# Windowed attention by pairs of neighbouring windows of one batch, with half the mask table and a loop of eight written-out steps

## Chip, cores and metric

One core of one Trainium2 chip runs the kernel. The metric is the device time of one execution in microseconds (us). Five engines work side by side, each through its own list of instructions: PE (TensorE: matmuls, and the weight loads shown as PEld), DVE (VectorE), ACT (ScalarE), POOL (GpSimd) and SP (SyncE, which here only issues DMAs). They order one another by semaphores.

## What is computed

The input x is (4, 32, 32, 128): four batches of 32 x 32 places with 128 channels. The first layer is a Swin block with windows of 8 x 8, shifted by 4, 16 heads of 8 channels, a rotary embedding, an additive mask per window, and a gated MLP. The second is a self-attention over all 1024 places of a batch.

```python
xw = windows(roll(layer_norm(x)))                  # 4 batches x 16 windows, 64 tokens each
q, k, v = rope(q(xw)), rope(k(xw)), v(xw)          # 16 heads of 8 channels
attn = softmax(q * scale @ k.T + attn_mask[window])   # mask depends on the window, not the batch
x = x + unroll(attn @ v @ proj_w.T + proj_b)
y = layer_norm(x)
x = x + (silu(gate(y)) * a(y)) @ fc2_w.T + fc2_b      # a, gate: halves of y @ fc1_w.T + fc1_b
f, g, h = x @ Wq + bq, x @ Wk + bk, x @ Wv + bv    # second layer, per batch, 1024 tokens
x = gamma * softmax(f @ g.T) @ h + x
```

The host rolls the image and cuts it into windows before the launch, and puts it together again after it.

## The kernel before

Two windows, 128 tokens, fill the 128 partitions; such a pair is the unit of the window attention. There are 32 pairs. Pair n holds window n // 2 of two batches (0 and 1 for an even n, 2 and 3 for an odd one). Both halves of a pair have the same window and so the same mask: `mask_f` holds the masks of all 16 windows for both directions of the scores, twice over the partitions (1,024 KB), and `mask16` is its bf16 form. A part of the mask that bf16 doesn't hold would go through two further parts of `mask16`; which of two written-out versions of PE's program runs (three parts or one) is decided by a value that PE loads at step -1, in two `pe.If` blocks. For the mask of this problem it is the second block, with one part.

**Stage 1, window attention.** Steps n = -2 to 34, one function `body(n, it, r)` for each engine (PE's has a count of mask parts besides). A step works on several pairs at once: PE projects q and k of pair n+2 (`project`, lines 748 and 750), turns q and k of pair n+1 (`turn`, line 786), writes the masks of pair n into two PSUM banks by a matmul with the identity (`masked`, line 758) and adds its scores (line 767), does masks and turned scores of pair n-1 (lines 758 and 779), multiplies pair n-3 with its values (line 843), projects v of pair n-1, and turns q of pair n once more with the row maxima in it (`t2`, line 786). DVE rotates q and k (line 941), copies the turned rows to `qk_t` (line 955), takes the row maxima (line 973), writes them as two f16 parts (lines 978 and 980) and normalises. ACT does the exponential and the f16 halves, POOL the low halves. SP sends the turned keys of the next pair to `k_t` in four DMAs, one after the other (line 717), as soon as DVE's copy is done; the scores of that pair wait for the last one (`kz_ready`).

The steps -2 to 3 are written out, the steps 4 to 27 are a hardware loop (`Fori`) of six turns of four written-out steps, and the steps 28 to 34 are written out again. In the loop an index that depends on n is a register; the mask's index is one of them, since the window is n // 2, and so is the pair that is projected. Behind the steps -1 to 3 lies the rest of the first layer norm (`ln_turn`, `ln_hi_of`, `ln_lo_of`, `ln_stats_of`, in chunks of four pairs). At the end of step -1 PE computes the bias of fc1 by 16 small matmuls (`bias`, line 444), which wait for the nine loads of REST; DVE adds to it at the start of its step 0 (line 539), and PE's step 0 begins by waiting for that.

**Loads.** SP issues three chunks of x (256 KB each), the mask table, five more chunks of x, and the nine loads of REST (line 707), of which `bv` is last.

**Stage 2, MLP.** Chunks of 512 tokens, which are four pairs. So a chunk of before has two windows of all four batches. ACT moves the result of a chunk to `x2_all` (line 578), whose layout is batch, window, token: it writes four pieces, one to each batch.

**Stage 3, second attention.** `project_fg(b, h)` (line 1356) computes the two sets of rows of half h of batch b from `x2_all`. ACT (`high_rows`, line 1641) and DVE (`rows_of`, line 1521) make them f16, and `other_half` (line 1337) sends them across the partitions: SP sends side 0 of batch 0, ACT side 1, after its `high_values`. The first scores (line 1389) wait for all four. PE's order before is fg(0,0), fg(1,0), a wait for all chunks of x2, fg(0,1), fg(1,1), then the values of batch 0 (line 1361, `project_v`).

Of the kernel before, what the change touches and what calls it, by code (L numbers as in the profile page):

```python
# [13 lines left out]
F32 = mybir.dt.float32  # L14
# [7 lines left out]
WIN, SHIFT = 8, 4  # L22
HEADS, HD = 16, 8
NWIN = (H // WIN) * (W // WIN)
WTOK = WIN * WIN
PAIRS = NWIN * B // 2
TOK = B * H * W
CHUNK = 512
CHUNKS = TOK // CHUNK
# [17 lines left out]
def at(start, size):  # L47

    return bass.ds(start, size)


def build(nc, t):
    ctx = ExitStack()
    with ctx:
# [59 lines left out]
        warm2 = sb("warm2", [128, 1])  # L114

        until_mlp = ExitStack()
        mask_f = until_mlp.enter_context(nc.sbuf_tensor("mask_f", [128, 2, NWIN, WTOK], F32))
        mask16 = until_mlp.enter_context(nc.sbuf_tensor("mask16", [128, 3, 2, NWIN, WTOK], BF16))
# [428 lines left out]
        def mlp_act(act):  # L547
# [26 lines left out]
            def body(c, u):  # L574
                if in_range(c, 2):

                    act.wait_ge(mlp_done, c - 1)
                    act.activation(x2_all[:, :, at(c * 2 - 4, 2), :],
                                   ps[:, OUT_BANK, :].rearrange("p (w b q) -> p b w q", w=2, b=B),
                                   ACT.Identity, bias=cols[:, 0:1], scale=1.0 / (WSCALE * WSCALE)).then_inc(x2_done, 1)  # L580
                if in_range(c, 1):
                    gate(c - 1, 0)
                    if isinstance(c, int) and c == 1:
                        high_of_a(2, 0)
                    gate(c - 1, 1)
# [44 lines left out]
        with ExitStack() as st:  # L630
            def tmp(name, shape, dt=F32):
                return st.enter_context(nc.sbuf_tensor(name, shape, dt))
# [9 lines left out]
            mrest = tmp("mrest", [128, 2, NWIN, WTOK])  # L642
# [17 lines left out]
            pv_ps = ps[:, PV_BANK, 0:HP * 4 * (HD + 1)].rearrange("p (h e r d) -> p h e r d", h=HP, e=2, r=2)  # L660

            FIRST, LAST = -2, PAIRS + 2
            LOOP_FROM, LOOP_TO = 4, PAIRS - 4

            LN_BANK = (PV_BANK, ST_BANK, ST_BANK + 1, PV_BANK, ST_BANK, PV_BANK, PV_BANK, PV_BANK)
            LN_BANK_FREE = (0, 0, 0, 1, 2, 4, 6, 7)
# [3 lines left out]

            def first_steps(body):
                for n in range(FIRST, 0):
                    body(n, n // 2, n % BUFS)

            def other_steps(eng, body, mlp_early):
                for n in range(0, LOOP_FROM):
                    body(n, n // 2, n % BUFS)
                with eng.Fori(LOOP_FROM // BUFS, LOOP_TO // BUFS) as it:
                    for r in range(BUFS):
                        body(it * BUFS + r, it * 2 + r // 2, r)  # L680
                for n in range(LOOP_TO, LAST + 1):
                    body(n, n // 2, n % BUFS)
                    mlp_early(LAST - n)

            def steps(eng, body, mlp_early):
# [10 lines left out]
            @block.sync  # L696
            def _(sp):
                for c in range(CHUNKS):
                    sp.dma_start(x_all[:, TPC * c:TPC * c + TPC, :],
                                 t["x"][:, TPC * c:TPC * c + TPC, :]).then_inc(x_loaded[c], 16)  # L700
                    if c == 2:

                        sp.wait_ge(qkv_loaded, 48)
                        sp.wait_ge(turn_loaded, 16)
                        sp.dma_start(mask_f[:], t["mask"]).then_inc(mask_loaded, 16)
                for dst, name in REST:
                    sp.dma_start(dst[:], t[name]).then_inc(rest_loaded, 16)
                sp.wait_ge(rows_set, 4)
                sp.wait_ge(keys_set, 1)

                def body(n, it, r):
                    if valid(n, -1):

                        sp.wait_ge(qt_ready, n + 2)
                        for j in range(4):
                            rows = slice(ROWS * j, ROWS * j + ROWS)
                            sp.dma_start(k_t[rows, (r + 1) % BUFS, j], qk_t[rows, (r + 1) % 2, 1]).then_inc(kz_ready[(r + 1) % 2], 16)

                steps(sp, body, nothing)

            @block.tensor
            def _(pe):
# [30 lines left out]
                def masked(bank, w, side, parts):  # L753

                    for part in range(parts):
                        for b in range(2):
                            mm = mask16[:, part, side, at(w, 1), :].broadcast_to([128, 8, WTOK])
                            pe.matmul(ps[:, bank + b, :].rearrange("p (h k) -> p h k", h=8), identb[:], mm,  # L758
                                      start=(part == 0), stop=False, skip_group_check=True)

                def scores(queries, keys, w, parts):

                    masked(S_BANK, w, 0, parts)
                    for c in range(4):
                        for e in range(2):
                            rows = slice(64 * e, 64 * e + 64)
                            last = pe.matmul(  # L767
                                ps[rows, S_BANK + c // 2, 256 * (c % 2):256 * (c % 2) + 256]
                                .rearrange("p (h k) -> p h k", h=4),
                                queries[:, c, rows], keys[:, :, c, rows], start=False, stop=True, skip_group_check=True)  # L770
                    return last
# [15 lines left out]
                                            ident16[:])  # L787
                    return last

                def body(n, it, r, parts):  # L790
                    u = r % 2
                    v = 1 - u

# [22 lines left out]
                    if valid(n, 0):  # L816

                        pe.wait_ge(kz_ready[u], it * 64 + 64)
                        wait(pe, mlo_done, n)
                        scores(qk_t[:, u, 0], k_t[:, r], it, parts).then_inc(s_done, 1)  # L820
                    if at_step(n, 0):
                        ln_turn(3)
                        ln_turn(4)
# [5 lines left out]
                    if valid(n, 1):  # L829

                        wait(pe, q2_ready, n)
                        wait(pe, exp_done, n - 1)
                        scores_turned(k_t[:, (r - 1) % BUFS], q_t2[:, v], it if u else it - 1, parts).then_inc(st_done, 1)
                    if at_step(n, 1):
                        ln_turn(5)
                    if valid(n, 3):
                        wait(pe, plo_done, n - 2)
                        wait(pe, norm_done, n - 3)
                        pe.wait_ge(ln_ready, CHUNKS)
                        for hp in range(HP):  # L840
                            out = pv_ps[:, hp].rearrange("p e r d -> p (e r d)")
                            for k, (p, w) in enumerate(((p_hi, v_hi), (p_hi, v_lo), (p_lo, v_hi))):
                                last = pe.matmul(out, p[:, v, 2 * hp:2 * hp + 2, :].rearrange("p h q -> p (h q)"),  # L843
                                                 w[:, v, hp].rearrange("p e r d -> p (e r d)"),
                                                 start=(k == 0 and hp == 0), stop=(k == 2), skip_group_check=True)
                        last.then_inc(pv_done, 1)
                    if valid(n, 1):
# [26 lines left out]
            def _(dve):  # L874
# [52 lines left out]

                dve.wait_ge(attn_loaded, 16 * len(ATTN))

                def body(n, it, r):  # L930
                    u = r % 2
                    v = 1 - u
                    if isinstance(n, int) and n == 0:
# [73 lines left out]
            def _(act):  # L1007
# [38 lines left out]
                ln_norm_of(2)  # L1046
                ln_hi_of(1)

                def body(n, it, r):
                    u = r % 2  # L1050
                    v = 1 - u
                    if isinstance(n, int):
# [62 lines left out]
            def _(pool):  # L1115
# [28 lines left out]

                pool.wait_ge(rows_set, 4)

                def body(n, it, r):
                    u = r % 2
                    k = (r + 2) % BUFS
                    if valid(n, -2):  # L1150
# [49 lines left out]


        until_mlp.close()
        x2_all = sb("x2_all", [128, B, NWIN, WTOK])
# [74 lines left out]
        with ExitStack() as st:  # L1278
# [31 lines left out]

            def fg_count(b, h):

                return 2 * h + b + 1 if b < 2 else 2 * b + h + 1

            def fg_bank(b, h):
                return (PV4 + 2 * b + h) if b < 2 else AUX
# [33 lines left out]
            def _(pe):  # L1350

                def tokens(b, first, count):
                    return x2_all[:, b].rearrange("p w q -> p (w q)")[:, first:first + count]
# [155 lines left out]
            def _(dve):  # L1509
# [86 lines left out]
                for h in range(2):  # L1596
                    for b in range(2):
                        rows_of(b, h)
                for h in range(2):
                    low_values(0, h)  # L1600
# [32 lines left out]
            def _(act):  # L1633
# [18 lines left out]
                for h in range(2):  # L1652
                    for b in range(2):
                        high_rows(b, h)
                high_values(0, 0)
                high_values(0, 1)
# [133 lines left out]
```

## Time and profile before

| | us |
|---|---|
| median of three runs | 422.26 |
| lowest and highest | 419.81, 424.24 |
| the profiled execution, its own time | 421.29 |
| its span from the first to the last instruction | 419.5 |
| stage 1 with its start | 0 to about 200 |
| of it the steps of the hardware loop | 50.3 to 167.6 |
| stage 2 without its overlap with stage 1 | about 200 to 288.5 |
| stage 3 | 288.5 to 419.5 |

Of the span PE is busy for 87%, DVE 73%, ACT 66% and POOL 62%. A busy share is a mean over stages with different limits; what ends a step has to be read from the step. Times below are from the start of the span.

### The profile page before, as it was taken

To read this page: it belongs to the slowest core of one execution; us is meant where nothing else is said; L and a number is where in the kernel's file an instruction comes from. 1 tells how busy PE (TensorE), PEld (TensorE's weight loads), DVE (VectorE), ACT (ScalarE), POOL (GpSimd) and SP (SyncE) were. 2 spreads that over 40 slices of the span, in tenths; PEclk is the share of its full clock that TensorE was granted. 3 is DMA by queue.
4 is the path that set the end of the run, shared out by engine and by line. 5 is a ranking of instruction groups with operands and counts; after the bars stand their busy time and mean duration, and the time that the engine had idled before them with its cause. 6 is when DMAs were issued, how large, how long until landed. Compare 5 with 4: busy or idle time off the path is not lost.

```text
span 419.5 us, 12535 instructions
## 1 busy us (share of the span) xinstructions
PE 363.6 (87%) x4732; PEld 229.6 (55%) x4732; DVE 307.5 (73%) x850; ACT 275.2 (66%) x436; POOL 259.1 (62%) x313
## 2 busy tenths in 40 slices
PE   2678799999999999978799999999269998989693
PEld 0455455666665666655355555545025766767563
DVE  8767688888888888887476666645787688784524
ACT  2758787777787778878355555455116866768581
POOL 6656476777777777886656666572006775857521
PEclk9999999999999999999899999999757999999989
DMA  6701001111000101100000000000100002010101
GB/s 199 253 22 26 18 27 27 28 28 30 26 25 25 28 26 30 29 16 3 1 2 2 0 0 0 2 0 9 45 0 15 14 19 58 3 50 2 43 11 51
DMA packets 15581, 12.53 MB, mean 30 GB/s; under 512 B 3991, under 2 KB 14136, under 8 KB 15416
## 3 DMA queue, kind: packets, MB, share of 16 engines
q1 hardware_dynamic: 14144, 11.42, 9.4%
q10 hardware_dynamic: 1400, 0.61, 0.6%
q8 instruction: 24, 0.39, 0.4%
q14 instruction: 13, 0.11, 0.1%
HBM read 4.68 MB, written 2.10 MB: 16 GB/s over the span
## 4 chain that ended last, share of the span: by engine, by line
PE 55%; DVE 20%; issue 7%; ACT 6%; POOL 4%; DMA 4%; SPq 3%; ACTq 0%; DVEq 0%; POOLq 0%
PE ps L334 8%; PE ps L1417 7%; PE ps L786 5%; PE ps L758 5%; DVE mx L1553 4%; PE ps L748 4%; PE ps L843 3%; PE ps L1361 3%; PE ps L779 3%; PE ps L767 3%; DVE ps L973 3%; POOL hl L275 2%; DVE ob L1591 2%; PE ps L750 2%; PE ps L1400 2%
## 5 line engine op out<-in xcount | busy, mean ns | idle before, releaser
L1679 POOL TENSOR_TENSOR el<-e,eh 128x1024 f16<-128x1024 f32 x28 | 59.6, 2130 | 65.2 <-ACT eh L1671 65.0
L1162 POOL TENSOR_TENSOR p_lo<-e_buf,p_hi 128x1024 f16<-128x1024 f32 x32 | 68.2, 2132 | 4.9 <-ACT p_hi L1017 3.6
L1664 ACT ACTIVATE e<-ps 128x1024 f32<-128x1024 f32 x32 | 32.7, 1023 | 39.0 <-PE ps L1406 38.7
L334 PE MATMUL ps<-y_t,fc_w 128*128 128x512 f16 x192 | 44.4, 387 | 3.7 <-POOL al L260 2.5
L1154 POOL TENSOR_TENSOR rot<-ta,tb 128x256 f32<-128x256 f32 x32 | 23.3, 728 | 38.9 <-DVE tb L941 38.7
L1553 DVE TENSOR_REDUCE mx<-ps 128x1 f32<-128x1024 f32 x32 | 39.1, 1221 | 9.9 <-PE ps L1390 9.6
L1417 PE MATMUL ps<-val,eh 128*128 128x129 f16 x512 | 37.7, 223 | 6.4 <-DVE ob L1591 5.7
L758 PE MATMUL ps<-mask,identb 128*128 (+1 forms) x128 | 39.0, 386 | 2.8 <-DMA k_t<-qk_t 2.1
L973 DVE TENSOR_REDUCE ps<-ps 128x16 f32<-128x1024 f32 x32 | 39.4, 1232 | 2.7 <-PE ps L767 1.8
L1081 ACT ACTIVATE e_buf<-ps 128x1024 f32<-128x1024 f32 x32 | 32.8, 1025 | 12.9 <-PE ps L779 12.8
L1417 PEld LDWEIGHTS ps<-val,eh 128*128 128x128 f16 x512 | 32.4, 99 | 15.0 <-issue 8.4
L456 DVE SCALAR_TENSOR_TENSOR hid<-ps,fc_bias,sg 128x512 f32<-128x512 f32 x32 | 23.9, 747 | 15.5 <-ACT sg L551 9.8
L1017 ACT ACTIVATE p_hi<-e_buf 128x1024 f16<-128x1024 f32 x32 | 33.9, 1059 | 0.8
L1671 ACT ACTIVATE eh<-e 128x1024 f16<-128x1024 f32 x32 | 33.8, 1055 | 0.7
L275 POOL TENSOR_TENSOR hl<-hid,hh 128x512 f16<-128x512 f32 x24 | 27.5, 1157 | 10.3 <-DVE yn L485 8.3
L334 PEld LDWEIGHTS ps<-y_t,fc_w 128*128 128x128 f16 x192 | 18.6, 99 | 25.2 <-POOL al L260 3.0
L748 PE MATMUL ps<-qkv_w,xn_all 128*128 128x128 f16 (+1 forms) x192 | 27.4, 252 | 4.5 <-issue 2.9
L551 ACT ACTIVATE sg<-ps,fc_bias 128x512 f32<-128x512 f32 x32 | 22.0, 689 | 13.3 <-PE ps L334 12.1
L786 PE MATMUL ps<-ident,q_rows 128*128 128x128 f16 x256 | 25.8, 224 | 4.7 <-DVE q_rows L980 3.5
L1017 ACT ACTIVATE q_t<-ps 128x512 f16<-128x512 f16 x32 | 19.1, 598 | 12.8 <-PE ps L786 12.6
L779 PEld LDWEIGHTS ps<-q_t,k_t 128*64 128x64 f16 x1024 | 18.7, 112 | 13.6 <-issue 13.6
L941 DVE TENSOR_TENSOR ta<-ps,rope 128x256 f32<-128x256 f32 x32 | 13.6, 424 | 14.3 <-PE ps L750 14.3
(158 smaller groups left out, 981.7 us busy)
## 6 DMA issues: line engine op xcount, KB each, us to landing
k_t<-qk_t SPq DMA_DIRECT2D x128, 32.0 KB, 1.8
x_all<-in_x SPq DMA_DIRECT2D x8, 256.0 KB, 5.6
out<-ob SPq DMA_DIRECT2D x8, 192.0 KB, 2.1
mask_f<-in_mask SPq DMA_DIRECT2D x1, 1024.0 KB, 4.8
yr<-xr SPq DMA_DIRECT2D x14, 64.0 KB, 2.0
fc_w<-in_fc_w SPq DMA_DIRECT2D x1, 512.0 KB, 6.8
out<-ob SPq DMA_DIRECT2D x4, 128.0 KB, 1.8
fc_w<-in_fc_w SPq DMA_DIRECT2D x1, 256.0 KB, 6.6
```

The costliest lines, as they stand in the source:

```text
L275: pool.tensor_tensor(hl[:, k, :], hid[:, k, :], hh[:, k, :], ALU.subtract).then_inc(hl_done, 1)
L334: last = pe.matmul(ps[:, bank, :], fc1_w16[:, ws, 128 * block_:128 * block_ + 128], y_t[:, v, ys, :], start=(n == 0), stop=(n == 2))
L748: pe.matmul(out, xn_all[:, at(i, 1), xs, :].rearrange("p a q -> p (a q)"), qkv_w16[:, ws, cols], start=(n == 0), stop=False, skip_group_ch ...
L758: pe.matmul(ps[:, bank + b, :].rearrange("p (h k) -> p h k", h=8), identb[:], mm, start=(part == 0), stop=False, skip_group_check=True)
L786: last = pe.transpose(out[:, c, :], rows[:, 4 * c:4 * c + 4, :].rearrange("p h r -> p (h r)"), ident16[:])
L973: dve.tensor_reduce(mx_ps, ps[:, S_BANK:S_BANK + 2, :].rearrange("p b (h k) -> p (b h) k", h=8), AX.X, ALU.max).then_inc(max_done, 1)
L1017: return act.activation(out, in_, ACT.Copy)
L1162: pool.tensor_tensor(p_lo[:, u], e_buf[:, u], p_hi[:, u], ALU.subtract).then_inc(plo_done, 1)
L1417: return pe.matmul(pv4[:, j, i, 0:DIM + 1], weights[:, T % H_BUFS, 128 * n:128 * n + 128], val[:, b % 2, part, m, 0:DIM + 1], start=first, ...
L1553: dve.tensor_reduce(mx[:, k:k + 1], two(s_bank(k)), AX.X, ALU.max, negate=True).then_inc(max4_done, 1)
L1671: act.activation(eh[:, T % H_BUFS, :], e4[:, T % E_BUFS, :], ACT.Copy).then_inc(eh_done, 1)
L1679: pool.tensor_tensor(el[:, T % H_BUFS, :], e4[:, T % E_BUFS, :], eh[:, T % H_BUFS, :], ALU.subtract).then_inc(el_done, 1)
```

## The change

A pair now holds the windows 2w and 2w+1 of one batch: pair n is batch n // 8, window pair n % 8. The mask table has eight places instead of sixteen; partitions 0 to 63 hold the mask of the even window and 64 to 127 of the odd one. Its load is 512 KB, its bf16 copy on ACT (line 1017) has 1024 elements a partition in place of 2048, and DVE's reduction over it (line 925) 512 in place of 1024.

So that the mask's index is a constant in the loop, the loop has eight written-out steps: steps -2 to 7 are written out, steps 8 to 23 are two turns of eight steps, and steps 24 to 34 are written out. This holds for all five engines, and for both versions of PE's program.

A chunk of the MLP is now 512 tokens of one batch in their order, so ACT writes one piece to `x2_all`. PE's order at the start of stage 3 becomes fg(0,0), fg(0,1), fg(1,0), the wait for all chunks, fg(1,1), and the orders of ACT, DVE and the counts follow.

```diff
-PAIRS = NWIN * B // 2
+WPAIRS = NWIN // 2
+PAIRS = WPAIRS * B
-        mask_f = until_mlp.enter_context(nc.sbuf_tensor("mask_f", [128, 2, NWIN, WTOK], F32))
+        mask_f = until_mlp.enter_context(nc.sbuf_tensor("mask_f", [128, 2, WPAIRS, WTOK], F32))
...
-                    act.activation(x2_all[:, :, at(c * 2 - 4, 2), :],
-                                   ps[:, OUT_BANK, :].rearrange("p (w b q) -> p b w q", w=2, b=B),
+                    act.activation(x2_all[:, at((c - 2) * CHUNK, CHUNK)], ps[:, OUT_BANK, :],
...
-            LOOP_FROM, LOOP_TO = 4, PAIRS - 4
+            LOOP_FROM, LOOP_TO = WPAIRS, PAIRS - WPAIRS
...
-                with eng.Fori(LOOP_FROM // BUFS, LOOP_TO // BUFS) as it:
-                    for r in range(BUFS):
-                        body(it * BUFS + r, it * 2 + r // 2, r)
+                with eng.Fori(LOOP_FROM // WPAIRS, LOOP_TO // WPAIRS) as it:
+                    for w in range(WPAIRS):
+                        body(it * WPAIRS + w, it * (WPAIRS // 2) + w // 2, w)
...
-                            mm = mask16[:, part, side, at(w, 1), :].broadcast_to([128, 8, WTOK])
+                            mm = mask16[:, part, side, w:w + 1, :].broadcast_to([128, 8, WTOK])
...
-                        scores(qk_t[:, u, 0], k_t[:, r], it, parts).then_inc(s_done, 1)
+                        scores(qk_t[:, u, 0], k_t[:, r], w, parts).then_inc(s_done, 1)
...
                 project_fg(0, 0)
+                pe.wait_ge(x1_ready, CHUNKS)
+                project_fg(0, 1)
                 pe.wait_ge(h_done, CHUNKS * HBLK)
                 project_fg(1, 0)
                 pe.wait_ge(x2_done, CHUNKS)
-                pe.wait_ge(x1_ready, CHUNKS)
-                project_fg(0, 1)
                 project_fg(1, 1)
...
-    x = x.reshape(B, nh, WIN, nw, WIN, DIM).transpose(1, 3, 0, 2, 4, 5).reshape(PAIRS, 2 * WTOK, DIM)
+    x = x.reshape(B, nh, WIN, nw, WIN, DIM).transpose(0, 1, 3, 2, 4, 5).reshape(PAIRS, 2 * WTOK, DIM)
...
-        "mask": np.concatenate([both, both], 0),
+        "mask": np.concatenate([both[:, :, 0::2], both[:, :, 1::2]], 0),
```

## Rows read from the trace of the kernel before

**Rows 1.** Windows (stretch, length, busy us of each engine, clock, DMA): the loop.
```profile
89.90:167.60 77.70, 76.39 (x1408) 48.22 (x1409) 67.36 (x176) 61.90 (x112) 58.52 (x79) 1.00 0.10 27
```

**Rows 2.** Timeline of PE (start, length): first matmuls of steps 8 to 12, 28, 29.
```profile
70.43 0.50 PE L748 MATMUL ps<-qkv_w,xn_all 128*128 128x256 f16 x3
75.27 0.50 PE L748 MATMUL ps<-qkv_w,xn_all 128*128 128x256 f16 x3
80.03 0.50 PE L748 MATMUL ps<-qkv_w,xn_all 128*128 128x256 f16 x3
84.80 0.50 PE L748 MATMUL ps<-qkv_w,xn_all 128*128 128x256 f16 x3
89.95 0.50 PE L748 MATMUL ps<-qkv_w,xn_all 128*128 128x256 f16 x3 [0.31 <-issue]
...
167.61 0.49 PE L748 MATMUL ps<-qkv_w,xn_all 128*128 128x256 f16 x3
...
172.28 0.49 PE L748 MATMUL ps<-qkv_w,xn_all 128*128 128x256 f16 x3
```

**Rows 3.** Waits in the window 70.4 to 167.6: us in total, times, longest.
```profile
PE ps L748 <- issue: 1.2, 4, 0.3
```

**Rows 4.** Timeline of PE: the mask matmuls of a loop step, then of step 29.
```profile
95.89 0.59 PE L758 MATMUL ps<-mask,identb 128*128 x2
...
173.44 0.61 PE L758 MATMUL ps<-mask,identb 128*128 128x512 bf16 x2
```

**Rows 5.** DMA queues: instruction packets of the whole span, then of 50.3 to 70.4.
```profile
q8 instruction: 24, 0.39, 0.4%
...
q8 instruction: 3, 0.05, 1.0%
```

**Rows 6.** DMA queue in 57 to 58.5, and in 63 to 65; SP's timeline; the chain.
```profile
q8 instruction: 1, 0.02, 3.9%
...
q8 instruction: 1, 0.02, 3.1%
...
57.93 1.03 SPq L717 DMA_DIRECT2D k_t<-qk_t  x1
...
63.95 2.70 DMA k_t<-qk_t
```

**Rows 7.** SP's key DMAs (line 717) in the whole span: issue time in ns, landing.
```profile
L717 SPq DMA_DIRECT2D k_t<-qk_t x128: 507/591/1633, 18.9 to 180.9; - x128
...
DMA to landing us min/median/max: 1.8/1.8/3.3
```

**Rows 8.** Waits in 50.3 to 70.4, then in 167.6 to 190.
```profile
PE ps L758 <- DMA k_t<-qk_t: 0.6, 2, 0.3
...
PE ps L758 <- DMA k_t<-qk_t: 1.0, 2, 0.5
```

**Rows 9.** The window 10 to 15; the chain from 14 to 23.2; PE's and DVE's timelines.
```profile
10.00:15.00 5.00, 3.50 (x17) 1.75 (x15) 3.37 (x7) 4.41 (x12) 3.15 (x6) 1.00 1.00 363
...
14.21 5.11 DMA bv<-in_bv
19.36 3.58 PE ps L444 x16
...
23.04 0.18 DVE fc_bias L539
...
24.62 0.80 PE L748 MATMUL ps<-qkv_w,xn_all 128*128 128x256 f16 x3 [1.69 <-issue]
...
22.54 0.38 DVE L888 BATCH_NORM_AGGREGATE mv<-stats 128x2 f32<-128x6 f32 x4
```

**Rows 10.** Waits in 18 to 25.
```profile
PE ps L444 <- DMA bv<-in_bv: 1.3, 1, 1.3
```

**Rows 11.** The chain from the end of the MLP to the first scores.
```profile
288.49 3.44 PE ps L1356 x8
...
294.32 2.26 DMA yr<-xr
```

More of the change, by code:

```diff
@@ L116, in build @@
         until_mlp = ExitStack()
-        mask_f = until_mlp.enter_context(nc.sbuf_tensor("mask_f", [128, 2, NWIN, WTOK], F32))
-        mask16 = until_mlp.enter_context(nc.sbuf_tensor("mask16", [128, 3, 2, NWIN, WTOK], BF16))
+        mask_f = until_mlp.enter_context(nc.sbuf_tensor("mask_f", [128, 2, WPAIRS, WTOK], F32))
+        mask16 = until_mlp.enter_context(nc.sbuf_tensor("mask16", [128, 3, 2, WPAIRS, WTOK], BF16))
         xn_all = until_mlp.enter_context(nc.sbuf_tensor("xn_all", [128, PAIRS, 2, 128], F16))
@@ L641, in build @@
             xn = tmp("xn", [128, 4, CHUNK])
-            mrest = tmp("mrest", [128, 2, NWIN, WTOK])
+            mrest = tmp("mrest", [128, 2, WPAIRS, WTOK])
             ta = tmp("ta", [128, 2, 2, HEADS, HD])
@@ L672, in first_steps @@
                 for n in range(FIRST, 0):
-                    body(n, n // 2, n % BUFS)
+                    body(n, n // 2, n % WPAIRS)
             def other_steps(eng, body, mlp_early):
                 for n in range(0, LOOP_FROM):
-                    body(n, n // 2, n % BUFS)
-                with eng.Fori(LOOP_FROM // BUFS, LOOP_TO // BUFS) as it:
-                    for r in range(BUFS):
-                        body(it * BUFS + r, it * 2 + r // 2, r)
+                    body(n, n // 2, n % WPAIRS)
+                with eng.Fori(LOOP_FROM // WPAIRS, LOOP_TO // WPAIRS) as it:
+                    for w in range(WPAIRS):
+                        body(it * WPAIRS + w, it * (WPAIRS // 2) + w // 2, w)
                 for n in range(LOOP_TO, LAST + 1):
-                    body(n, n // 2, n % BUFS)
+                    body(n, n // 2, n % WPAIRS)
                     mlp_early(LAST - n)
@@ L709, in _, with body @@
                 sp.wait_ge(keys_set, 1)
-                def body(n, it, r):
+                def body(n, it, w):
+                    r = w % BUFS
                     if valid(n, -1):
@@ L788, in turn, with body @@
                     return last
-                def body(n, it, r, parts):
+                def body(n, it, w, parts):
+                    r = w % BUFS
                     u = r % 2
@@ L832, in body @@
                         wait(pe, exp_done, n - 1)
-                        scores_turned(k_t[:, (r - 1) % BUFS], q_t2[:, v], it if u else it - 1, parts).then_inc(st_done, 1)
+                        scores_turned(k_t[:, (r - 1) % BUFS], q_t2[:, v], (w - 1) % WPAIRS, parts).then_inc(st_done, 1)
                     if at_step(n, 1):
@@ L841, in body @@
                             out = pv_ps[:, hp].rearrange("p e r d -> p (e r d)")
-                            for k, (p, w) in enumerate(((p_hi, v_hi), (p_hi, v_lo), (p_lo, v_hi))):
+                            for k, (p, vals) in enumerate(((p_hi, v_hi), (p_hi, v_lo), (p_lo, v_hi))):
                                 last = pe.matmul(out, p[:, v, 2 * hp:2 * hp + 2, :].rearrange("p h q -> p (h q)"),
-                                                 w[:, v, hp].rearrange("p e r d -> p (e r d)"),
+                                                 vals[:, v, hp].rearrange("p e r d -> p (e r d)"),
                                                  start=(k == 0 and hp == 0), stop=(k == 2), skip_group_check=True)
@@ L928, in _, with body @@
                 dve.wait_ge(attn_loaded, 16 * len(ATTN))
-                def body(n, it, r):
+                def body(n, it, w):
+                    r = w % BUFS
                     u = r % 2
@@ L1047, in _, with body @@
                 ln_hi_of(1)
-                def body(n, it, r):
+                def body(n, it, w):
+                    r = w % BUFS
                     u = r % 2
@@ L1145, in _, with body @@
                 pool.wait_ge(rows_set, 4)
-                def body(n, it, r):
+                def body(n, it, w):
+                    r = w % BUFS
                     u = r % 2
@@ L1202, in build @@
         until_mlp.close()
-        x2_all = sb("x2_all", [128, B, NWIN, WTOK])
+        x2_all = sb("x2_all", [128, TOK])
         sg = sb("sg", [128, 2, CHUNK])
@@ L1311, in fg_count @@
             def fg_count(b, h):
-                return 2 * h + b + 1 if b < 2 else 2 * b + h + 1
+                return 2 * b + h + 1
             def fg_bank(b, h):
@@ L1352, in tokens @@
                 def tokens(b, first, count):
-                    return x2_all[:, b].rearrange("p w q -> p (w q)")[:, first:first + count]
+                    return x2_all[:, b * NB + first:b * NB + first + count]
                 def project_fg(b, h):
@@ L1594, in finish @@
                     last.then_inc(o_ready, 1)
-                for h in range(2):
-                    for b in range(2):
+                for b in range(2):
+                    for h in range(2):
                         rows_of(b, h)
@@ L1650, in high_values @@
                                    scale=VSCALE).then_inc(v4_hi, 1)
-                for h in range(2):
-                    for b in range(2):
+                for b in range(2):
+                    for h in range(2):
                         high_rows(b, h)
```

## The prediction

> **What bounds the kernel now.** I read the windows by stage first, since a share over the whole span mixes three stages. In the hardware loop PE is busy for 76.39 of 77.7 us while DVE, the next, has 67.36 [rows 1]; the granted clock is 1.00, the upper of its two levels (2.4 GHz). So the loop's time is PE's own work plus the few places where PE stands. The timeline shows them. Each step begins with the projection of q and k on line 748, and from one to the next it is 4.84, 4.76, 4.77 and 5.15 us, 19.52 for a turn of four [rows 2]. An undisturbed loop step is therefore 4.76 us. The fourth, behind which PE's program jumps back, is 0.39 longer, and the step after the jump 0.08 longer: a jump costs 0.47 us. The waits say the same: PE stood before line 748 four times, for 0.3 us each, and its releaser is "issue", so no other engine was late [rows 3]. The steps written out behind the loop start 4.67 us apart (167.61 to 172.28, rows 2): there PE has no jump and no index to work out.
>
> PE also stands where the turned keys come late. SP's four DMAs for a pair take 591 ns each to issue and the last lands 1.8 us after its start [rows 7], so keys are there some 4 x 0.6 + 1.8 = 4.2 us after SP begins, a little under a step. That chain has only some tenths of slack, and what disturbs it is seen in the rows: the instructions that PE runs come through a DMA queue of their own, in 24 packets of 0.39 MB together, 16 KB each [rows 5]. When one of them moved at 57 to 58.5, a key DMA took 1.03 us to issue; another was there in 63 to 65, and a key DMA started at 63.95 landed after 2.70 us [rows 6]. PE's waits for keys in 50.3 to 70.4 are 0.6 us in two times; behind the loop, where packets come again, 1.0 us in two times [rows 8]. Between 70.4 and 167.6 none of either is seen: the waits name no DMA and the queue has no packet, so the loop's four steps stay in the engine after the first turn. Three packets belong to 20.1 us of new code [rows 5], one for every 6.7 us, or 1.4 steps.
>
> **The change part by part.** The sum is made against the profiled execution, 421.29 us, which is 1.8 over its span of 419.5.
>
> *Jumps back.* Before there are five (ahead of steps 8, 12, 16, 20, 24), after there is one, ahead of 16. Four go. Three of them are like the one measured, 3 x 0.47 = 1.41. That ahead of step 8 has no "issue" in its row (70.43, rows 2), so I count half, 0.24. Gain 1.65 us. Bounds: nothing, if PE was waiting for others anyway, and 4 x 0.47 = 1.9.
>
> *The mask's index as a constant.* It removes register work ahead of line 758. But two mask matmuls take 0.59 us in the loop and 0.61 in the written-out step 29 [rows 4]. The work hides behind the queue of matmuls in front of it: nothing. The projection's index stays a register in the loop.
>
> *Eight steps that leave the loop* (4 to 7, 24 to 27). They lose the register work on line 748 as well: 4.76 - 4.67 = 0.09 each, 8 x 0.09 = 0.7 us, from a single pair of starts, so between 0 and 0.7; I take 0.6.
>
> *More code to bring in.* 12 more bodies of PE are passed for the first time (17 before, 29 after): 12 / 1.4 = 9 more packets, some 33 in all. They fall into the steps 8 to 15 and 24 to 27, where there are none now. Of the three in rows 5 two met SP's chain, at 0.6 / 2 = 0.3 us each; the phase moves by a third of a step from one packet to the next, so I take two of three again: 6 x 0.32 = 1.9 us lost. Bounds: 0, and 9 x 0.5 = 4.5 (the 1.0 us in two times of rows 8). This is the term that takes back what the jumps give.
>
> *The smaller mask table, at the start.* From 10 to 15 the 16 DMA engines are busy all the time at 363 GB/s [rows 9]; 0.52 MB less is 1.4 us. The last load, bv, now lands 5.11 us after its issue at 14.21, and PE's 16 bias matmuls begin at 19.36, having waited 1.3 us for it [rows 9, 10]. All 1.3 us go, as 1.4 is more. Behind them stand DVE's addition, ended at 23.04 + 0.18 = 23.22, and then 1.4 us up to the first matmul of step 0 at 24.62, of whose wait the releaser is "issue" [rows 9]. Here two readings part. If those 1.4 us are PE's jump into the second If block, which waits for no one, they move with PE, and step 0 begins 1.25 us earlier. If they begin with DVE's addition, little moves: DVE is in its statistics until 22.54 + 0.38 = 22.92 [rows 9] and can add only 0.1 us earlier. A plain hand-over costs a few hundredths (bv has landed at 19.32, PE starts at 19.36), so the jump is the likelier; the steps 0 to 3 then hang on PE's first scores and keep the shift. I take 1.2; bounds 0.1 and 1.3. ACT's copy of the mask and DVE's reduction, both of half the length now, lie beside ACT's wait for POOL's layer norm and DVE's for PE: nothing.
>
> *Stage 2.* The same 512 elements in one piece instead of four; ACT waits for PE's last matmuls before it. Nothing, within 0.1.
>
> *Stage 3, the new order of fg.* Before, the four projections run without a gap, 3.44 us from 288.49, 0.86 each [rows 11]; so the wait for all of x2 between them stops no one. What releases the first scores is ACT's second DMA of batch 0, started at 294.32 and landed 2.26 us later; it is behind ACT's high_values, which wait for project_v. That is behind four projections in either order. Nothing. SP's second DMA of batch 0 goes some 0.9 us earlier, beside that path.
>
> Sum: -1.65 - 0.6 + 1.9 - 1.2 = -1.55 us, 419.7 for an execution like the profiled one. The median before, 422.26, is 1.0 above that; the same step down from it is 420.7. The runs before lie between 419.81 and 424.24.
>
> **The rivals.**
>
> *Code that doesn't stay.* The four-step loop, three packets long, is kept by PE. Eight steps are 8 / 1.4 = 6 packets. If that is more than PE holds beside what it reads ahead, the jump at step 16 goes to code that isn't there. Its price is about that of the stop ahead of step 0, 1.69 us [rows 9], and the second turn's six packets cost 6 x 2/3 x 0.32 = 1.3. Then it is -1.55 + 1.7 - 0.5 (the plain jump) + 1.3 = +0.95: 423.2, slower than before. It decides as soon as more than about 1.6 us are lost in this way. For it: nothing shows that PE keeps more than three packets. Against it: the first turn of four brought nothing back five times. The Trainium skill (Runtime: NRT & Kernel Launch, "Instruction fetch mechanics") says that PE's instruction memory holds 128 KiB in blocks of 16 KiB, into which six blocks would fit; the same section says that a taken branch out of a window of two pages stops for a fetch, by which the loop of before, three packets, would have stopped at each jump. The queue without a packet from 70.4 to 167.6 speaks against that second sentence here. Chance 0.2.
>
> *Packets that don't meet SP's chain, and an earlier start that gives more.* Then the 1.9 us are 0.3. And the first three matmuls of step 0 take 0.80 us [rows 9] where the same three take 0.50 later [rows 2]; with a shorter stop of PE ahead of them this slow phase may end sooner, by as much as 1 us: -1.65 - 0.6 + 0.3 - 1.2 - 1.0 = -4.15, or 418.1. The trace has packets that met nothing. Chance 0.2.
>
> *The start doesn't move* (DVE's addition is what PE waits for) and the packets cost what I say: -0.45, 421.8. Chance 0.2.
>
> *The forecast*: 420.7, chance 0.4.
>
> **How the numbers follow.** The likeliest is 420.7. Below it the second rival reaches 418.1, and with the scatter of a median of few runs 417.5; above it the first gives 423.2, and with it 424.2. I give 417.6 to 424.0, which leaves about 2 in 10 outside. What can be told from no change is about 1%, 4.2 us: all cases but the end of the second rival lie within it. Faster by more than 1%: 0.11, half of the second rival. Slower by more: 0.05, the far end of the packets' bound or a second turn that stops on several engines. Within: 0.84.
>
> **What would show it.** The steps 17 to 23 begin every 4.76 us and 4.67 in 4 to 7 and 24 to 27 where no packet meets them; one stop of 0.3 us with "issue" on line 748, not four; 33 packets on the instruction queue (about 39 if the second turn fetches again, and then a stop of over 1 us at step 16); waits for keys in the steps 5 to 15 and 24 to 27, of about 0.3 us, six more than before. The bias matmuls begin near 18.1 and step 0 near 23.4 (24.5 if DVE releases it). From the first fg matmul to the landing of ACT's DMA it is 8.1 us as before. I'm wrong if a key wait costs far more or less than 0.3 us, if PE or another engine stops for code in the second turn, or if stage 2 or 3 moves by more than 0.5 us.

## The result: slower by 0.7%

Over 20 runs each, the median is 424.68 us (421.18 to 426.83) against 420.93 us (419.64 to 425.3) before; the ratio is 1.0073, 95% interval 1.005 to 1.0095. The ratio compares the means of the runs, and 0.73% of 421 us is 3.1 us; the medians lie 3.75 us apart. The forecast was 1.5 us less, with 420.7 us and 417.6 to 424.0 around it. The profiled execution of the changed kernel has a span of 421.6 us, 2.1 more than before.

The profile's page of the changed kernel: engines, granted clock in 40 slices, and the instruction queue.

```profile
PE 365.1 (87%) x4732; PEld 231.0 (55%) x4732; DVE 307.5 (73%) x850; ACT 273.6 (65%) x436; POOL 259.5 (62%) x313
...
PEclk9998999999999999999899999999658999999889
...
q8 instruction: 32, 0.52, 0.5%
```

The busy times hardly move: the work is the same. The instruction packets have gone from 24 to 32 [rows 5]. In the stretch from 70.4 to 167.6 PE has become idle for longer:

```profile
70.40:167.60 97.20, 92.62 (x1693) 58.24 (x1691) 83.09 (x215) 76.22 (x139) 71.55 (x98) 1.00 0.10 28
```

PE is idle for 4.6 us of 97.2 there; before, it was idle for 1.3 us of 77.7 [rows 1]. The timeline of PE gives the start of each step; these are the first matmuls of the steps 4, 6, 7, 8, 9, 11, 12, 13, 15, 16, 17, 18 and 28:

```profile
50.03 0.49 PE L749 MATMUL ps<-qkv_w,xn_all 128*128 128x256 f16 x3
...
60.26 0.49 PE L749 MATMUL ps<-qkv_w,xn_all 128*128 128x256 f16 x3
65.01 0.49 PE L749 MATMUL ps<-qkv_w,xn_all 128*128 128x256 f16 x3
70.11 0.49 PE L749 MATMUL ps<-qkv_w,xn_all 128*128 128x256 f16 x3
75.78 0.49 PE L749 MATMUL ps<-qkv_w,xn_all 128*128 128x256 f16 x3
...
85.28 0.50 PE L749 MATMUL ps<-qkv_w,xn_all 128*128 128x256 f16 x3
91.06 0.49 PE L749 MATMUL ps<-qkv_w,xn_all 128*128 128x256 f16 x3
96.51 0.49 PE L749 MATMUL ps<-qkv_w,xn_all 128*128 128x256 f16 x3
...
106.03 0.50 PE L749 MATMUL ps<-qkv_w,xn_all 128*128 128x256 f16 x3
111.80 0.50 PE L749 MATMUL ps<-qkv_w,xn_all 128*128 128x256 f16 x3
116.64 0.50 PE L749 MATMUL ps<-qkv_w,xn_all 128*128 128x256 f16 x3
121.40 0.50 PE L749 MATMUL ps<-qkv_w,xn_all 128*128 128x256 f16 x3
...
170.17 0.49 PE L749 MATMUL ps<-qkv_w,xn_all 128*128 128x256 f16 x3
```

The step from 65.01 on has 5.10 us, those from 70.11, 85.28, 91.06 and 106.03 have 5.67, 5.78, 5.45 and 5.77. Where nothing disturbs, a step of the loop takes what was foreseen: 116.64 to 121.40 is 4.76, and the steps 18 to 23 take 4.76 to 4.80. What the long steps have in common is a wait for keys. PE's waits for keys in 50 to 170.2:

```profile
PE ps L759 <- DMA k_t<-qk_t: 5.3, 7, 1.0
```

Seven waits, 5.3 us together, 0.75 each in the mean and 0.24 to 0.98 singly; in [rows 8] it was two, 0.3 each. At 83 the picture is the one of [rows 6], only larger. SP's timeline there, the instruction queue in 83 to 84.5, and from the chain the key DMA that PE waited for in three other pairs:

```profile
83.20 1.75 SPq L718 DMA_DIRECT2D k_t<-qk_t  x1
...
q8 instruction: 1, 0.02, 5.3%
...
34.73 3.38 DMA k_t<-qk_t
...
68.95 3.25 DMA k_t<-qk_t
...
89.23 3.71 DMA k_t<-qk_t
```

An issue of 1.75 us in place of 0.59, landings of 3.3 to 3.7 us in place of 1.8. The 2.1 us between the two spans can be accounted for by the steps' starts in both timelines: up to step 0 the changed kernel is 1.17 ahead; the steps 0 to 3 take 26.58 us instead of 25.72 (+0.86); the steps 4 to 27 take 120.14 instead of 117.27 (+2.87); from step 28 to the first fg matmul both take 120.7; from there to the end 130.8 instead of 131.2 (-0.4). So the whole loss of this execution lies in stage 1.

### The profile page after: what moved, and what is told of

The parts are those of the page before. It is cut to its first block, busy times and chain, and to the rows that moved or that the text cites. A ratio compares the mean times of both kernels' runs of the same rounds, so it can differ in the third digit from the quotient of the medians.

```text
span 421.6 us, 12328 instructions
## 1 busy us (share of the span) xinstructions
PE 365.1 (87%) x4732; PEld 231.0 (55%) x4732; DVE 307.5 (73%) x850; ACT 273.6 (65%) x436; POOL 259.5 (62%) x313
## 4 chain that ended last, share of the span: by engine, by line
PE 55%; DVE 20%; ACT 6%; DMA 5%; issue 5%; POOL 4%; SPq 3%; DVEq 0%; POOLq 0%; ACTq 0%
PE ps L335 9%; PE ps L1422 8%; PE ps L759 5%; DMA k_t<-qk_t 5%; PE ps L787 4%; DVE mx L1558 4%; PE ps L845 3%; SPq L718 3%; PE ps L780 3%; PE ps L768 3%; PE ps L1366 3%; PE ps L749 3%; POOL hl L276 2%; DVE ob L1596 2%; PE ps L349 2%
## 5 line engine op out<-in xcount | busy, mean ns | idle before, releaser
L759 PE MATMUL ps<-mask,identb 128*128 128x512 bf16 x128 | 39.4, 391 | 9.9 <-DMA k_t<-qk_t 9.1
L1085 ACT ACTIVATE e_buf<-ps 128x1024 f32<-128x1024 f32 x32 | 32.8, 1024 | 19.5 <-PE ps L780 18.1
L1422 PE MATMUL ps<-val,el 128*128 128x129 f16 x256 | 23.8, 226 | 0.1
```

The lines of the kernel that those rows point to most:

```text
L1422: return pe.matmul(pv4[:, j, i, 0:DIM + 1], weights[:, T % H_BUFS, 128 * n:128 * n + 128], val[:, b % 2, part, m, 0:DIM + 1], start=first, ...
```

## Experiments

Two theories stood at first. Theory P: instruction packets move at the same time as SP's key DMAs and make them late, and PE then waits 0.7 to 1 us. Rival L: the new pairs and layout cost the time. Later came rival S: PE stops for want of instructions, and the key waits only go along with it.

**The loop of eight alone, and the half table alone.**

```diff
# loop8: the kernel before, with
-            LOOP_FROM, LOOP_TO = 4, PAIRS - 4
+            LOOP_FROM, LOOP_TO = 8, PAIRS - 8
-                with eng.Fori(LOOP_FROM // BUFS, LOOP_TO // BUFS) as it:
-                    for r in range(BUFS):
-                        body(it * BUFS + r, it * 2 + r // 2, r)
+                with eng.Fori(LOOP_FROM // 8, LOOP_TO // 8) as it:
+                    for w in range(8):
+                        body(it * 8 + w, it * 4 + w // 2, w % BUFS)
# half4: the kernel before, with half the mask table, pair n = window pair n // 4 of batch n % 4
-    x = x.reshape(B, nh, WIN, nw, WIN, DIM).transpose(1, 3, 0, 2, 4, 5).reshape(PAIRS, 2 * WTOK, DIM)
+    x = x.reshape(B, nh, WIN, nw // 2, 2, WIN, DIM).transpose(1, 3, 0, 4, 2, 5, 6).reshape(PAIRS, 2 * WTOK, DIM)
-        "mask": np.concatenate([both, both], 0),
+        "mask": np.concatenate([both[:, :, 0::2], both[:, :, 1::2]], 0),
```

> The kernel before with the loop of eight steps alone: pairs, mask table (1,024 KB), chunk layout and the order of fg as before. Theory P (instruction packets meet SP's key DMAs, and one that does costs PE 0.7 to 1.0 us, not 0.3): the queue has about 32 packets instead of 24, of which some 8 meet a key DMA in the steps 4 to 27; the stretch from step 4 to step 28 is about 120 us instead of 117.3; step 0 stays at 24.6; in all 3 us more than before, ratio 1.006 to 1.010. Rival L (the new pairs or the one-piece layout cost the time, the loop of eight is what it seemed): four jumps fewer and no loss, 1.5 to 2 us less than before, ratio 0.996.

Measured: ratio 1.0042 (1.0015 to 1.007); 33 instruction packets; step 0 at 24.24; the steps 4 to 27 in 121.2 us. PE's waits for keys in these steps:

```profile
PE ps L758 <- DMA k_t<-qk_t: 5.3, 7, 1.1
```

The same seven waits and 5.3 us, with the old pairs, the old table and the old order. The ratio is a little under the 1.006 to 1.010 that theory P gave; rival L would have given 0.996.

> Pairs of neighbouring windows and the mask table of half the size, but the loop of four: pair n is window pair n // 4 of batch n % 4, so the mask's index stays one register, and a chunk keeps two windows of four batches. Theory P: 24 packets, steps in the loop 4.76 us with jumps of 0.47 as before, step 0 at 23.4 instead of 24.6, so up to 1.2 us less than before, ratio 0.997 to 1.000 (the lead of 1.2 may shrink before step 4, as it did to 0.3 with the change). Rival L: the pairs cost, ratio 1.004 or more.

Measured: ratio 0.9989 (0.9967 to 1.001), no difference that can be told; 24 packets; step 0 at 23.69, the steps 4 to 27 in 118.9 us with two key waits of 1.4 us together. The jumps cost 0.16 us more than before (a step of 5.30 where it was 5.14), which had not been foreseen. The pairs as such cost nothing that can be told; the loop of eight does. Between the two ratios lies 0.5%. Added up, the two parts give 1.003, and the whole change 1.0073; the difference is about what the three intervals together allow, and no run assigns it.

**The key DMAs by two queues.**

```diff
# in SP's body
-                        for j in range(4):
+                        for j in range(2):
# in ACT's body, behind its q and k halves
+                    if valid(n, -1):
+                        act.wait_ge(qt_ready, n + 2)
+                        for j in range(2, 4):
+                            rows = slice(ROWS * j, ROWS * j + ROWS)
+                            act.dma_start(k_t[rows, (r + 1) % BUFS, j], qk_t[rows, (r + 1) % 2, 1]).then_inc(kz_ready[(r + 1) % 2], 16)
```

> The changed kernel, with two of the four key DMAs of a pair issued by ACT behind its q and k halves, the other two by SP. Theory P: the chain from DVE's copy to the last landing is 1.2 us shorter, which is more than a packet takes from it, so PE's waits for keys in the steps 4 to 28 fall from about 7 us to under 1.5 with the same 32 packets, and the time falls by 5 us or more, to about 418 to 419, ratio 0.993 to 0.996 against before. Rival S (PE is starved of instructions by the packets themselves, the key waits only stand in for it): same packets, same time, 424 or so, ratio 1.007. ACT may lose 0.3 us a step in either case, beside other work.

Measured: ratio 1.0026 (0.9992 to 1.006). The forecast of 0.993 to 0.996 was missed. With the same 32 packets the steps 4 to 27 take 117.6 us instead of 120.1, half of the 5 us expected, and the key waits in them are 2.6 us, not under 1.5. The start took more away: ACT's first key DMAs stand in front of its copy of the mask, which PE waits for, and step 0 began at 25.18.

> The kernel before with the same split of the key DMAs. Theory P: little to win, since only the packets outside the loop meet keys there: the waits for keys of 0.6 us in steps 4 to 7 and 1.0 us behind the loop go, 1 to 1.6 us less, ratio 0.996 to 0.998. If ACT's part of the keys costs as such, it shows here: ratio 1.0 or above.

Measured: ratio 1.0034 (1.0008 to 1.006), a miss by the same start (step 0 at 26.0). In the steps 4 to 27 the time is 117.37 against 117.27: without packets in the loop the split has next to nothing to win.

So the split was put in only from step 3 on:

```diff
+            def split(n):
+                return not isinstance(n, int) or n >= 3
-                        for j in range(4):
+                        for j in range(2 if split(n) else 4):
-                    if valid(n, -1):
+                    if valid(n, -1) and split(n):
```

> The changed kernel with the key DMAs split between SP and ACT from step 3 on only; in the steps before that SP issues all four, since with the split from the first step on step 0 began at 25.2 instead of 23.5. Theory P: 32 packets as before, step 0 at 23.5, the steps 4 to 28 in 117.6 us as with the split everywhere instead of 120.1: 2.5 us less than the changed kernel, ratio against before 0.999 to 1.002. Theory S: 120.1 stays.

Measured: 420.07 us, ratio 0.9973 (0.9943 to 1.0002) against before, where the changed kernel has 1.0073; 0.999 to 1.002 was expected. The steps 4 to 27 take 117.8 us, with this left of the key waits:

```profile
PE ps L762 <- DMA k_t<-qk_t: 2.5, 4, 0.9
```

The number of packets and the program of PE are those of the changed kernel, so want of instructions (rival S) can't be what cost 2.3 us of 120.1; lateness of the keys was. The two ratios differ by 1.0%, 4.2 us, more than these 2.3. In the profiles the part behind step 28 is 2.3 us shorter too (249.2 instead of 251.5), but it is 249.3 in before_2q and 251.9 in the kernel before as well, so that part scatters by about as much from one execution to the next.

**A long packet without an instruction in it.** The loop of four brings in no code after its first turn, so the packet can be put in by hand, in the second of the four steps:

```diff
# packet
+                    if not isinstance(n, int) and r == 1:
+                        act.dma_start(extra[0:1, :], t["x"][0:1, :, :].rearrange("p a d -> p (a d)")).then_inc(extra_sent, 16)
# packet8k
+                    if not isinstance(n, int) and r == 1:
+                        act.wait_ge(ln_ready, CHUNKS)
+                        act.dma_start(xn[0:32].rearrange("p a q -> p (a q)"),
+                                      t["x"][0:32, 0:16, :].rearrange("p a d -> p (a d)")).then_inc(extra_sent, 16)
```

> The kernel before, whose loop of four brings in no instructions after its first turn; ACT starts one extra copy of 16 KB in one row (16 KB of x to a scratch row in DRAM) in the second step of each loop turn, while SP sends the keys. Nothing waits for it but a later step of ACT. If it moves as one packet on one DMA engine, theory P expects a key DMA that issues or lands 0.5 to 1.5 us later and a wait of PE for keys of 0.3 to 1.0 us in each of the six turns, which are then up to 20.4 us instead of 19.5, without any instruction packet there. Theory S (PE stops for lack of instructions) expects 19.5.

Measured: it did not become the packet it was meant to be. The queue of ACT has 192 packets more for the six copies, 32 each, of which 16 hold 1 KB and 16 hold 4 bytes; so the 16 KB went in small pieces. The turns stayed at 19.5 to 19.6 us and there was no key wait in them from 70 on. As a test of a long packet it says nothing; it shows that another 16 KB in packets of 1 KB does no harm here.

> The same with the 16 KB as 16 rows of 1 KB, so that they can lie on 16 DMA engines. Theory P (it is the length of one packet on one engine that holds up the keys): no key waits, turns of 19.5 to 19.6 us. If the mere start of another DMA from ACT's queue holds SP's up, it is as in the run before.

Measured: 192 packets more as well, turns of 19.5 us, no key wait from 71 on. In effect the same run.

> The kernel before, and in the second step of each loop turn one extra copy by ACT of 32 rows of 8 KB (256 KB) into a tile that is no longer read: 32 packets of 8 KB, two for each of the 16 DMA engines, each engine thus occupied for about as long as by one instruction packet of 16 KB. The two runs with 16 KB in packets of 1 KB left the turns at 19.5 us. Theory P (a long packet ahead of a key packet on its engine is what makes keys late): each of the six turns gets a key wait of PE of 0.5 to 1.5 us, turns of 20 to 21 us, though no instruction packet moves in them. Theory S (PE stops for instructions, not for keys): 19.5.

Measured: each of the six turns has a key wait; the first five turns take 21.2, 20.8, 20.7, 20.7 and 20.7 us, the last 22.0, and the span is 426.9 us. PE's waits in the steps 4 to 27, a landing from the chain, and the DMA queues in 76 to 170, which have no line of an instruction queue:

```profile
PE ps L759 <- DMA k_t<-qk_t: 7.6, 6, 1.6
...
80.67 3.25 DMA k_t<-qk_t
...
q1 hardware_dynamic: 3585, 2.45, 9.9%
q10 hardware_dynamic: 240, 1.31, 5.4%
```

Long packets of data do to the keys what the instruction packets did: a landing of 3.25 us, waits of 1.07 to 1.60. The last turn's extra length is not one of the keys: its wait is 1.34 us like the others, but the granted clock falls behind it, as told in the last section. This run moves 256 KB in 32 packets at a time, so its size can't be carried over to one packet of 16 KB; its direction can. Nor were the 256 KB sent in small packets for comparison, so that the length of the packets and not the amount is what counts is argued, not shown.

**More code still.** The changed kernel with all steps written out:

```diff
-                for n in range(0, LOOP_FROM):
+                for n in range(0, LOOP_TO):
                     body(n, n // 2, n % WPAIRS)
-                with eng.Fori(LOOP_FROM // WPAIRS, LOOP_TO // WPAIRS) as it:
-                    for w in range(WPAIRS):
-                        body(it * WPAIRS + w, it * (WPAIRS // 2) + w // 2, w)
```

> The changed kernel with all steps -2 to 34 written out for all engines, no loop in stage 1. Theory P: 8 more bodies, so 6 more packets (38), of which 3 to 4 meet keys at 0.75 us each, less the last jump (0.3) and 0.08 for each of 16 steps (1.3): 1 to 1.5 us more than the changed kernel, about 425 to 426; the steps 16 to 23, which had no key wait, get three or four. Rival L (loops are what costs): less time than the changed kernel, by 1.6 us.

Measured: ratio 1.0063 (1.0022 to 1.0105), 38 packets. The steps 4 to 27 take 120.1 us, the same as in the changed kernel, with three waits more, but smaller ones (0.56 us in the mean):

```profile
PE ps L756 <- DMA k_t<-qk_t: 5.6, 10, 1.0
```

The sum in these steps shows no loss: six more packets cost about as much as the shorter undisturbed steps (4.68 and 4.75 us by turns, 4.76 in the loop) and the last jump give back. The forecast of 1 to 1.5 us more than the changed kernel is neither borne out nor refuted by a ratio with this interval; nor is the rival's 1.6 us less.

> All steps written out and the split key DMAs from step 3 on. Theory P: 38 packets, but of key waits only 2 to 3 us are left, as with the split and the loop of eight; steps of 4.68 without jumps: the steps 4 to 28 in 116 us instead of 120.1, ratio against before 0.993 to 0.998. Theory S: 120 as without the split.

Measured: ratio 1.0045 (1.0019 to 1.007), a miss. The key waits fell to 1.7 us, but PE now waits 2.3 us for POOL's `k_rows`, and the steps 4 to 27 take 118.0 us, not 116. It seems that ACT's share of the key DMAs delays what POOL waits for; steps of 4.68 and 4.75 us seem to leave no room for it, which was not tried further.

> Half the mask table with the loop of four and 24 instruction packets, and the split key DMAs from step 3 on. It should have both small gains, the start (0.7 us at step 4) and no key waits behind step 4 (1.5 us), less 0.8 us of slower jumps: 1.5 us less than before, ratio 0.995 to 0.998, no better than the changed kernel with the split by more than 1 us.

Measured: 420.31 us, ratio 0.9973 (0.9952 to 0.9995), as expected: the steps 4 to 27 in 117.9 us with one key wait of 0.7 us. It and the changed kernel with the late split have the lowest ratios of all; neither is apart from the other, nor clearly from half4 alone (0.9989).

> The changed kernel with the old order at the start of stage 3 (fg(0,0), fg(1,0), fg(0,1), fg(1,1), and ACT, DVE and counts with it). Every theory: from the first fg matmul to the first scores 8.2 to 8.4 us as in both kernels, the rest as the changed kernel.

Measured, in a single execution: from the first fg matmul to the first scores 8.2 us (294.55 to 302.77), and 8.25 in the changed kernel. The order of fg is neutral. That execution took 427.22 us; 1.9 us of it came with a step 4 of 7.47 us instead of 5.55, of which the last section has more.

## Why the prediction was wrong

**Jumps and constant addresses: right.** Only one jump is left. The steps written out take 4.68 us (now and then 4.75), those in the loop 4.76, as in [rows 2], and the constant mask index made no difference to either. The second turn of eight steps runs through at 4.76 to 4.80, behind a first step of 4.84 us, with no instruction packet, so the code stayed, and the rival that it doesn't fell. The Trainium skill (Runtime: NRT & Kernel Launch, "Instruction fetch mechanics") gives PE 128 KiB; six blocks of 16 KiB staying agree with that, and the same section's stop at a jump out of a window of two pages is not seen at step 16.

**The number of packets: right.** 33 were forecast, 32 came. Twelve of them start between 48.0 and 164.4, and seven met the keys; two of three were forecast.

**The price of a packet: wrong, and this is the step that failed.** The mechanism was the forecast one; the term "6 x 0.32 = 1.9 us lost" was too small. I took 0.32 us from the two waits in [rows 8], and 0.5 us as its upper bound. It measured 0.75 us in the mean of seven, which is the sign of being wrong that I had named. These are the two waits, in PE's timeline before:

```profile
61.61 0.60 PE L758 MATMUL ps<-mask,identb 128*128 x2 [0.34 <-DMA k_t<-qk_t]
...
66.69 0.61 PE L758 MATMUL ps<-mask,identb 128*128 x2 [0.30 <-DMA k_t<-qk_t]
```

They were poor witnesses. The first followed an issue longer by only 0.44 us, which leaves 0.1 us for the slack of the chain. The second came right behind it: its keys were 0.8 us late, but PE was already late by 0.34 and so gave them more time. The rows I had showed the real size: an issue of up to 1,633 ns instead of 591 and a landing of up to 3.3 us instead of 1.8 [rows 7]. These longest ones fell at 39 and at 21, where PE did not wait for keys but was held up elsewhere, so no wait showed them. The delay less the slack, 0.9 to 1.4 us, is the upper bound I should have kept. With the price as measured the term is 7 x 0.75 = 5.3, less the 0.6 that before had already, 4.7 in place of 1.9, which is over the 4.5 of my bound too; and my own sum for the steps 4 to 27 is -1.65 - 0.6 + 4.7 = +2.4 us, near the measured +2.87.

The recorded sum for the chain is wrong as well. It adds four issues and a landing, 4.2 us, but the landing is counted from the start of the last issue, so it is three issues and a landing, 3 x 0.6 + 1.8 = 3.6 us; in the undisturbed steps of the loop it measures 3.67. That would have left half a microsecond more of room, and yet there is next to none: in the loop before, the keys of pair 13 are there at 95.83 and the mask matmul that waits for them starts at 95.89 (those of pair 12, behind a jump, have 0.46 us). So the length of the chain says nothing of its slack; the distance from landing to use does.

**What I had not counted: step 2.** In 30 to 40 one packet and two of another instruction queue move, and the keys of pair 2, of which one DMA went at 34.73, landed 3.38 us later; PE waited 2.1 us instead of 0.55. Then the granted clock fell, as told in the last section. Even so step 2 is only 0.50 us longer (8.62 instead of 8.12), since before PE stood 1.86 us for the layer norm at its end, and that stop is gone. With step 3 (+0.23) and step 1 (+0.13) the steps 0 to 3 took 0.86 us more, and the lead from the start shrank by that.

**The start: right in size by luck, wrong in reason.** I forecast 1.2 us from bv's earlier landing and put ACT's copy of the mask at nothing. Step 0 did begin 1.17 us earlier. ACT's timeline and PE's, for the changed kernel and for the one with the split keys (after_2q), each with the copy of the mask and the first matmuls of step 0:

```profile
18.48 1.04 ACT L1020 ACTIVATE mask<-mask_f 128x1024 bf16<-128x1024 f32 x1
23.45 0.80 PE L749 MATMUL ps<-qkv_w,xn_all 128*128 128x256 f16 x3 [1.44 <-DVE fc_bias L543]
```

```profile
20.43 1.06 ACT L1020 ACTIVATE mask<-mask_f 128x1024 bf16<-128x1024 f32 x1 [1.86 <-issue]
25.18 0.80 PE L749 MATMUL ps<-qkv_w,xn_all 128*128 128x256 f16 x3 [3.08 <-issue]
```

Step 0 follows the end of that copy by 3.9 and 3.7 us here, by 4.2 before (20.40 and 24.62), by 3.9 with the loop of eight alone (20.37 and 24.24), and by 3.7 in before_2q (22.34 and 26.0); half4 has 4.2 and after_2q_late 4.3. Each time an instruction packet starts about 1 us after the copy: 21.4 before, 20.6 after, 22.5 and 23.4 with the split from the first step on. In the program PE waits for the copy (`mask_hi`) and then jumps into the second If block; the packet's time suggests that it brings in the code there while it still works on the 16 small matmuls. So it was the end of the copy, 0.9 us shorter and begun at the same time (18.48 and 18.50), that moved the jump. The shorter load gave nothing that can be seen. The distance from copy to step 0 varies by 0.6 us, which is not explained. That DVE's addition would hold step 0 up was nearly so: the addition ends at 23.17 and PE starts at 23.45.

**Stage 2 and 3: right.** From step 28 to the first fg matmul it is 120.7 us both times; from the first fg matmul to the landing of ACT's DMA 8.0 us, 8.1 before [rows 11]. The chain after:

```profile
291.05 3.44 PE ps L1361 x8
294.49 1.80 PE ps L1366 x16
...
296.92 2.09 DMA yr<-xr
```

**The range.** It ended at 424.0 and the median is 424.7. It stood on the median of three runs before, 422.26; over 20 runs that median is 420.93, and the forecast change of -1.55 from there gives 419.4. So the forecast time is off by 4.0 us and the forecast change by 4.6. The account of the profiled execution gives 2.1 us of the 3.1. The rest is not settled by a trace. The mean granted clock is 0.955 over the 20 runs after and 0.961 over the 35 runs of before beside loop8, and within each set the slower runs are those with the lower clock (correlation -0.8 and -0.7), which fits; whether the lower clock makes a run slow or goes with it was not tried.

## What to carry to other kernels

Writing a loop out further removes jumps (0.3 to 0.6 us each here) and brings in code by packets of 16 KB; where a small DMA is due in every step with little slack, a packet that meets it may cost more than a jump did (0.75 us here). Before unrolling, look for the steps that already run new code, and read the longest issue and landing there and not the waits that happened to follow. Then give the late transfer slack first. A DMA moved to another engine's queue is in front of whatever that engine does next, so look at its first use as well as at its steady state.

## What was not expected of the hardware

In a stop of 1.3 to 2.5 us, or within 1.7 us behind it, PE's granted clock can fall to its lower level for some 3 us. Windows of the changed kernel, around the key wait of 2.1 us that ends at 38.16, and of the kernel before around its stop of 1.86 us that ends at 43.54:

```profile
37.00:39.40 2.40, 1.24 (x10) 0.47 (x10) 0.82 (x3) 2.36 (x6) 1.04 (x2) 0.92 0.11 28
39.40:42.40 3.00, 3.00 (x42) 2.02 (x41) 2.38 (x4) 2.18 (x6) 2.51 (x4) 0.50 0.08 22
42.40:46.00 3.60, 3.60 (x36) 2.21 (x36) 0.76 (x2) 3.51 (x6) 0.96 (x2) 1.00 0.00 0
```

```profile
42.40:46.00 3.60, 2.46 (x26) 1.69 (x26) 1.45 (x3) 3.54 (x7) 1.01 (x4) 1.00 0.03 9
```

0.50 is 1.2 GHz of 2.4. All fourteen profiles but one have such a fall between 37 and 57; the one without is that of the kernel before. Eight of the others have it beside a stop for the layer norm of 1.85 us (half4 and packet among them), and the kernel before has the same stop, of 1.86 us, without it. In packet8k it is as uneven with the key waits, here at 84 and at 167, with the window behind the second:

```profile
84.05 0.60 PE L759 MATMUL ps<-mask,identb 128*128 x2 [1.32 <-DMA k_t<-qk_t]
...
166.91 0.99 PE L759 MATMUL ps<-mask,identb 128*128 x2 [1.34 <-DMA k_t<-qk_t]
...
167.00:170.40 3.40, 3.40 (x36) 1.30 (x35) 1.43 (x2) 0.36 (x2) 2.62 (x4) 0.50 0.14 39
```

Two waits of the same length, and only the second was followed by the slow clock: two mask matmuls then take 0.99 us instead of 0.60, and the turn 22.0 us instead of 20.7. So the length of the stop alone does not decide it in these runs. What a fall costs depends on whether PE is what the step waits for. It cost about 1.3 us in that turn. In step 4 of after_fg (7.47 us instead of 5.55) it goes with 1.4 us, when the longer key wait of 0.55 is taken off. In step 3 it cost nothing: 6.33 and 6.34 us in half4 and packet with the fall, 6.34 before without it.

The second thing: a key DMA beside an instruction packet of 16 KB is late in two places, at its issue by SP (up to 1.75 us instead of 0.59) and in its landing, counted from the start of its issue (3.3 to 3.7 us in the rows above instead of 1.8). The late landing was also seen beside data packets of 8 KB.
